# Zeroed rows from 112 partitions, single-batch scatters, and late weights loaded in portions, in a two-layer Flamingo block with two expert stages

## What is computed

```
x = x + tanh(g_xattn[0]) * masked_cross_attention(layernorm(x), ctx)     # 16 heads of 16
x = x + tanh(g_ffn[0])   * moe(layernorm(x))      # shared MLP + top 2 of 8 experts, F = 192
x = x + tanh(g_xattn[1]) * cross_attention(layernorm(x), ctx)
x = x + tanh(g_ffn[1])   * lora_ffn(layernorm(x)) # F = 1024, the top 1 of 8 low-rank corrections
```

## Time and profile before

| | |
|---|---|
| median of 3 runs | 944.09 us (935.59 to 944.37) |
| the profiled execution's own time | 942.44 us |
| its span | 940.4 us |
| PE busy | 789.5 us, 84% |
| DVE busy | 584.5 us, 62% |
| ACT busy | 469.9 us, 50% |
| POOL busy | 223.2 us, 24% |
| mean granted TensorE clock | 0.923 of full speed |
| moved by DMA | 118.91 MB, 126 GB/s over the span |

### The profile page before, as it was taken

The page is one execution under the profiler, slowest core; times in us unless marked ns, Lnnn a source line. Parts: engine busy times, 40 slices in busy tenths (PEclk is TensorE's granted clock), DMA queues, the critical chain, the costliest instruction groups (busy, mean ns, idle before and its releaser), DMA issues.

```text
span 940.4 us, 22247 instructions
## 1 busy us (share of the span) xinstructions
PE 789.5 (84%) x7992; PEld 612.4 (65%) x7992; DVE 584.5 (62%) x1773; ACT 469.9 (50%) x1004; POOL 223.2 (24%) x213
## 2 busy tenths in 40 slices
PE   5479999999989878604999858999999999878996
PEld 3247777776767655403899526767777777547996
DVE  4867777777767556501544547877888877663332
ACT  3336565564545346201566225655666665634543
POOL 2535222343233126001000535423231212000000
PEclk9789999999989789856999978999999999989998
DMA  7966788787767622112332696888879887000001
GB/s 198 227 167 137 159 173 163 150 176 172 136 135 158 158 66 81 49 48 61 98 123 92 186 189 137 171 179 167 193 152 181 167 178 146 10 2 1 18 18 35
DMA packets 152137, 118.91 MB, mean 126 GB/s; under 512 B 80844, under 2 KB 143608, under 8 KB 152024
## 3 DMA queue, kind: packets, MB, share of 16 engines
q1 hardware_dynamic: 144960, 107.35, 51.7%
q0 software_dynamic: 4096, 6.57, 2.6%
q10 hardware_dynamic: 2976, 3.61, 1.3%
HBM read 77.84 MB, written 39.40 MB: 125 GB/s over the span
## 4 chain that ended last, share of the span: by engine, by line
PE 62%; DMA 10%; DVE 9%; SPq 7%; issue 5%; ACT 4%; POOL 1%; another core or an unknown queue 0%; DVEq 0%; ACTq 0%; POOLq 0%
PE ps L1885 18%; PE ps L1998 8%; PE ps L2024 8%; PE ps L2047 6%; PE ps L2057 6%; SPq L610 4%; PE ps L2043 3%; DMA cT<-in_ctxT 3%; PE ps L2081 3%; DVE mx L1513 2%; DMA scr_x<-yt 2%; DMA QS<-scr_q 2%; DMA QS<-mp 1%; ACT prob L950 1%; PE ps L2067 1%
## 5 line engine op out<-in xcount | busy, mean ns | idle before, releaser
L950 ACT ACTIVATE prob<-ps 128x400 f32<-128x400 f32 (+1 forms) x384 | 183.0, 500 | 109.3 <-PE ps L2047 94.5
L2024 PE MATMUL ps<-KS,QS 96*100 96x361 bf16 x512 | 168.0, 343 | 24.3 <-DVE mx L1509 10.5
L1509 DVE CUSTOM_DVE_ANT_0 ps<-ps,biasq 100x361 f32<-100x361 f32 x256 | 135.9, 543 | 68.8 <-PE ps L2024 59.2
L1513 DVE TENSOR_REDUCE mx<-ps 100x1 f32<-100x361 f32 x256 | 127.0, 527 | 49.5 <-PE ps L2024 44.2
L2047 PEld LDWEIGHTS ps<-QS,KS 98*128 98x128 bf16 x1536 | 110.6, 101 | 51.7 <-issue 11.9
L2047 PE MATMUL ps<-QS,KS 98*128 98x100 bf16 x1536 | 135.1, 212 | 6.6 <-ACT prob L950 4.6
L1998 PE MATMUL ps<-cT,wk 128*128 128x361 f32 x256 | 102.5, 512 | 19.5 <-DMA ident<-in_ident 9.7
L2024 PEld LDWEIGHTS ps<-KS,QS 96*100 96x100 bf16 x512 | 65.1, 128 | 61.1 <-DVE mx L1509 17.7
L2057 PE MATMUL ps<-prob,V 128*17 128x100 f32 (+1 forms) x3072 | 82.6, 257 | 1.8 <-ACT xT L860 0.9
L689 POOL TENSOR_TENSOR kp<-kr,kp 128x722 bf16<-128x722 f32 x32 | 48.4, 1514 | 150.1 <-ACT kp L921 150.1
L2057 PEld LDWEIGHTS ps<-prob,V 128*17 128x17 f32 (+1 forms) x3072 | 67.0, 100 | 15.9 <-issue 10.8
(11 more groups left out here) (226 smaller groups left out, 1630.8 us busy)
## 6 DMA issues: line engine op xcount, KB each, us to landing
scr_k<-kp SPq DMA_DIRECT2D x96, 180.5 KB
KS<-scr_k SPq DMA_DIRECT2D x64, 270.8 KB, 3.6
cT<-in_ctxT SPq DMA_DIRECT2D x32, 361.0 KB
KS<-scr_k SPq DMA_DIRECT2D x64, 180.5 KB, 4.0
QS<-scr_q SPq DMA_DIRECT2D x64, 150.0 KB, 4.4
KS<-scr_k SPq DMA_DIRECT2D x64, 90.2 KB, 4.1
scr_q<-qp SPq DMA_DIRECT2D x24, 200.0 KB, 3.6
scr_q<-qp SPq DMA_DIRECT2D x48, 100.0 KB, 5.0
```

Of the source, the lines that this page charges most:

```text
L950: nc.scalar.activation(prob[0:KROWS[t], t, hg, :], ps[0:KROWS[t], c % 2, 0:HQ * S], ACT.Exp).then_inc(a["exp"], 1)
L1509: nc.vector.tensor_tensor_reduce(ps[0:S, banks[h % len(banks)], 0:S2], ps[0:S, banks[h % len(banks)], 0:S2], biasq[p][:, :], 1.0, -3.0e38, ...
L1513: nc.vector.reduce_max(mx[:, h:h + 1], ps[0:S, banks[h % len(banks)], 0:S2], axis=AX.X).then_inc(a["max"], 1)
L2024: mm(ps[0:S, banks[h % len(banks)], 0:S2], QS[p][0:SROWS, h, :], KS[p][0:SROWS, h * S2:(h + 1) * S2], start=True, stop=True).then_inc(a["s ...
```

## The change

The zeroed rows are written from 112 partitions with 3 rows each (336 rows) in place of 82 with 4 (328), and regions are 16 rows longer. `later_weights` moves behind `zero_fill` on SP. `scatter` takes one batch (two transfers). Batches 0 to 7 go out in POOL's loop for n = 8 to 15, each behind a wait for the end of step n-2, and `k3(n+1)` moves ahead of `biasT_(n)` in every round of the loop. The loads of `wiT`, `woT` and `BT` leave ACT; SP issues them in portions in steps 2 to 8 of attention 1 (two of 512 KB, four of 256 KB, then three of 128 KB), between the first half of the query load and `max_load`. `combine(1)` moves behind the last item. The counts that wait for the last weights follow (`NWF1`).

```diff
-REGION = B * S + TM
+REGION = B * S + TM + 16
...
-        ZROWS = 2 * S + TM
-        ZPART = 82
+        ZPART = 16 * 7
+        ZROWS = 3 * ZPART
+        NWF1 = 3 + KT + NFT1 // 2 + LPROD
...
+            def last_weights(b):
+
+                if b < KT:
+                    sp.dma_start(wiT[:, b, :], io["wiT"][b * P:(b + 1) * P]).then_inc(s_wf[1], 16)
+                elif b < KT + NFT1 // 2:
+                    t = 2 * (b - KT)
+                    sp.dma_start(woT[:, t:t + 2, :], io["woT"].rearrange("(t p) n -> p t n", p=P)[:, t:t + 2, :]).then_inc(s_wf[1], 16)
+                elif b == KT + NFT1 // 2:
+                    for r in range(LPROD):
+                        sp.dma_start(BT[r * LR:(r + 1) * LR, :], io["loraBT"]).then_inc(s_wf[1], 16)
+
...
                         expert_down(weights, u)
+                    if l == 1 and b >= 2:
+                        last_weights(b - 2)
                     max_load(l, b + 1, 1 - u)
...
                 max_load(l, B - 1, 1)
-                if l == 0:
-                    later_weights()
...
             zero_fill()
+            later_weights()
             sp.wait_ge(s0["tab"], START + NTAB)
...
                     for n in range(2, B):
-                        if n % 2 == 1 and n >= 9:
-                            scatter((n - 9) // 2)
                         bias(n, n % 2, n // 2, False)
-                        biasT_(n, n % 2, False)
+                        if n >= 8:
+                            pool.wait_ge(sa[0]["sT"], START + 3 * NHG * (n - 1))
+                            scatter(n - 8)
                         if n + 1 < B:
                             k3(l, n + 1)
+                        biasT_(n, n % 2, False)
                         if n % 2 == 0 and n >= 4:
                             norm_pair(F0, n // 2 - 2)
                     norm_pair(F0, NPAIR - 2)
-                    for j in range(NPAIR - 4, NPAIR - 1):
-                        scatter(j)
+                    for b in range(B - 8, B - 2):
+                        scatter(b)
...
-            scatter(NPAIR - 1)
+            for b in range(B - 2, B):
+                scatter(b)
...
-            act.wait_ge(s0["y"], START + NI)
-            act.dma_start(wiT[:, :, :], io["wiT"].rearrange("(k p) n -> p k n", p=P)).then_inc(s_wf[1], 16)
-            act.dma_start(woT[:, :, :], io["woT"].rearrange("(t p) n -> p t n", p=P)).then_inc(s_wf[1], 16)
-            for r in range(LPROD):
-                act.dma_start(BT[r * LR:(r + 1) * LR, :], io["loraBT"]).then_inc(s_wf[1], 16)
             attn(1)
...
                         combine(0)
-                        combine(1)
                 if b == NI:
+                    combine(1)
                     pair_stats(0)
```

More of the change, by code:

```diff
@@ L805, in low_piece, with scatter @@
                 nc.gpsimd.tensor_tensor(lo, raw, hi.bitcast(F32), ALU.subtract).then_inc(s0["plo"], 1)
-            def scatter(j):
+            def scatter(b):
+                j = b // 2
                 pool.wait_ge(s0["rt"], START + routed(j + 1))
@@ L811, in scatter @@
                     pool.wait_ge(s_zero, 16 * (1 + E))
-                for b in (2 * j, 2 * j + 1):
-                    for c in range(2):
-                        nc.gpsimd.indirect_dma_start(scr_x, bass.IndirectOffsetOnAxis(posi[:, c, b:b + 1], 0),
-                                                     normalized(b), None).then_inc(s_scat, 16)
+                for c in range(2):
+                    nc.gpsimd.indirect_dma_start(scr_x, bass.IndirectOffsetOnAxis(posi[:, c, b:b + 1], 0),
+                                                 normalized(b), None).then_inc(s_scat, 16)
             attn(0)
@@ L1079, in attn @@
                         else:
-                            act.wait_ge(s_wf[1], 16 * (5 + LPROD))
+                            act.wait_ge(s_wf[1], 16 * NWF1)
                             high(s1, *EARLY[0][:2])
@@ L1962, in logits @@
                 if g == 0:
-                    pe.wait_ge(s_wf[1], 16 * (5 + LPROD))
+                    pe.wait_ge(s_wf[1], 16 * NWF1)
                 pe.wait_ge(sn["xT"], START + NORMS[2 * l + 1] + g + 1)
```

## The result

The changed kernel takes **900.64 us** (median of 4 runs, 894.97 to 903.28) against 942.97 for the kernel before beside it: a ratio of 0.9561, with a 95% interval of 0.9501 to 0.9621. The profiled execution took 903.28 us (span 901.4, mean granted clock 0.951), 39.2 less than that of before. The forecast was 886, range 873 to 904. Faster is right, and the time lies inside the range, but 15 us of the forecast 57 are missing.

The account below looks back on a forecast made before the run. One transfer shape on about two DMA engines bounds the stretch near 400 us, PE and its ring of waits the rest. Terms -43.6 - 12 - 1.5 - 2 - 1 + 3 = -57.1 from 942.4 give 885.3, stated as 886 us, range 873 to 904.

Parts of the forecast that it names:

- The zero fill: Before the first tile: zeroed rows land sooner, PE's 44.58 us gap shrinks to 1.0 us; -43.6 us.
- issue-bound: SP's queue: with 112 partitions on all engines, eight fills cost only issue and register reads, 13.8 us.
- The scatters: Attention 0, steps 7 to 14: two scatters as a step opens instead of four in mid-step; -12 us.
- the burst's excess: Attention 0, steps 7 to 13: 17.8 us over quiet steps, between all and none recoverable, two thirds taken.
- paid by count: Rival: every POOL transfer delays its neighbours equally wherever it stands, so the 12 us stay; 898 us, chance 0.13.
- The row taken as nearest: Attention 1: POOL issues gather pairs at the same place with no "remote" waits; basis for taking two thirds.
- The stall as step 15 opens: End of attention 0: PE's 4.52 us standstill shrinks as `later_weights` leaves that spot; -1.5 us, between 0 and -4.5.
- The start of attention 1: Moving `combine(1)` lets PE start earlier, -2 us; final weights leaving that stretch, -1 us.
- The portions: Attention 1, seven steps: 2.4 MB of final weights may delay `max_load`; +3 us, between 0 and +12.6.
- weights gone: Start of attention 1: 2.4 MB of final weights leave a stretch with DMA engines 1.00 busy; -1 us (0 to -5).
- `later_weights` behind the fill: SP's queue before the first tile: its loads land while POOL scatters; 0, at worst tiles 4.7 us later.
- what would show it: The prediction's list of signs in fills, first-tile gap, clock, attention steps and waits that would show it right or wrong.

Follow-up runs that it names:

- e1_fill: Kernel before with only the new zero fill (112 partitions, regions 16 rows longer): 875.04 us against 920.31 for the kernel before, ratio 0.9522.
- e6_84: Kernel before with its zero fill cut as 84 partitions of 4 rows instead of 82: 902.07 us against 939.00 (one run).
- e8_fill_late: Kernel before with the new fill, and the final weights in portions at the end of a step's loads: 897.71 us against 939.00, ratio 0.9560.
- e4_act: Changed kernel with the final weights loaded whole by ACT as attention 1 begins: 875.63 us against 920.31 for the kernel before, ratio 0.9536.
- e3_out: Changed kernel with all scatters moved behind the loop of steps of attention 0: 896.21 us against 920.31 for the kernel before (one run).
- e10: Changed kernel with k3 first, scatters after the last weighting, and final weights loaded whole by ACT: 876.25 us against 920.69, ratio 0.9511.
- e2_pv: Changed kernel with a step's two scatters waiting for the ended batch's last weighting, not its last transposed score: 884.96 us against 920.31, ratio 0.9630.
- e9: Changed kernel with k3 first on POOL, then the scatters after the ended batch's last weighting: 879.55 us against 920.69, ratio 0.9571.
- e5_again: Changed kernel run once more, unedited, in another set: 897.06 us against 939.00 for the kernel before, ratio 0.9559.
- e7_late: Changed kernel with the portions of the final weights asked for at the end of a step's loads: 901.84 us against 939.00, ratio 0.9592.
- e11_again: Changed kernel run a third time, unedited: 880.87 us against 918.68 for the kernel before, ratio 0.9500.

## Why the prediction was right, and where it was not

**The zero fill (-43.6 forecast): right.** Alone it is worth 45.3 us by the medians (e1_fill), and the stretch to the first tile is 47.2 shorter in the two traces. The step that carries it, that 112 partitions make the fill issue-bound, holds: eight fills took 9.95 us and not 13.8, since an issue is 0.58 and not 0.88 us and the rest of a fill 0.76 and not 0.85. The steps behind it fit by luck. The forecast had the landing release POOL at 382.6 and a gap of 1.0 us left on PE. In fact POOL started at 382.65 for its places, which were ready 1.2 us later than before, and no gap was left, since PE came free 1.0 us later too. Most of the other 2.6 us of the 47.2 is the clock, which the prediction left unpriced at up to 2: from the first tile to its down projection (9.2 us before, 6.8 now) it was 0.71 and is 1.00.

**The scatters (-12 forecast): wrong, +1.1 measured.** The step that failed is "the burst's excess": 17.8 us over quiet steps were read as a clash of four scatters in mid-step with the normalising instruction, of which two thirds would go. The place of the excess was read rightly: it lies in the steps with scatters, and DVE's and ACT's "remote" waits are part of it. What failed is that a change of order would take it away. The same instructions of before cost 136.4, 134.6 or 128.6 us in the costly sets and 121.3 in another, the changed ones 138.0 and 136.1 or 122.8. The kernel before and the changed kernel were both in the costly condition when they were compared, so the 15 us were there to see and were not gained. In the costly sets a scatter costs whichever order it stands in; the new order only moves the standstill from DVE, ACT and PE in mid-step to PE at the weighting. Within one set the old order is never the slower one: 136.4 against 138.0, 134.6 and 128.6 (e6_84, e8_fill_late) against 136.1 and 136.5, and 121.3 against 123.3 for e4_act's. The rival "paid by count" fits the first pair of traces, with (136.4 - 121.3) / 16 = 0.9 us a scatter in the old order and (138.0 - 122.8) / 14 = 1.1 in the new, and its 898 us are nearer to the 900.64 than the forecast. But e8_fill_late paid half of that in a costly set, and in the other sets the count costs next to nothing, at most 0.15 us a scatter (e4_act against e3_out). The row taken as nearest, the gathers of attention 1, said rightly that such a pair can be free, but nothing in one trace tells that its stalls are not the kernel's own.

**The stall as step 15 opens (-1.5): right in size, not in its reason.** It shrank by 0.8 in the row and by 1.0 in the stretch. But the move of `later_weights` isn't shown to have done it: in the costly sets the stall is 3.0 to 4.5 us with the loads there (before, e6_84, e8_fill_late) and 3.0 to 4.4 without them, and in the other sets it is 0.6 us in every kernel, e1_fill among them, which still has them there.

**The start of attention 1 (-3 for `combine(1)` and the weights): right in the row, not in the time.** PE's first projection came 0.51 us after its last item, 2.6 us better. But the normalised queries came later by 1.4 us (they waited for `xn`), and the stretch to the first transpose shrank by 0.4. Over the kernels, this stretch and attention 1 together take 280.1 to 282.6 us with `combine(1)` in its old place and weights whole (before, e1_fill, e6_84), and 281.4 and 282.3 with it moved (e4_act, e10): 0 us for the move. The first stretch alone is some 3 us shorter with it (37.8 and 38.0 against 40.7 to 41.5), as forecast, and attention 1 some 3 us longer (243.7 and 244.3 against 238.6 to 241.6). The prediction's own caution, that the gathered rows set the first queries, was priced at half a microsecond and took 1.4; why the rest comes back in attention 1 is open.

**The portions (+3): right in kind, low.** Kernels with whole weights take 280.1 to 282.6 us for the two stretches, five of them, mean 281.7; kernels with portions ahead of `max_load` take 282.9 to 289.7, seven of them, mean 286.4. That is +4.7, within the bounds of 0 and 12.6, and net of what the "weights gone" from the start bought (-1 forecast). It is a mean over sets: within one set the difference was 4.2 us (e2_pv and e3_out against e1_fill and e4_act), 3.2 (e9 against e10) and 0.3 (e5_again against e6_84), and the changed kernel by itself gave 288.5, 282.9 and 288.1 in its three traces. The mechanism named, the landing of the maxima behind the portion, shows at 3.69 and 3.35 us in the place of 1.93, but it is one of several: in e7_late the wait for the context grows instead.

**`later_weights` behind the fill (0): right**; e1_fill and e11_again both take 27.8 us to the first tile.

**Together:** -45 to -47 for the fill, +4.7 for the portions, +1 for the scatters, -1 for the stretch with the stall, 0 for the rest, some -41 against the -42.3 measured. The tail's +2.5 in the balance is no part of it: the kernels' tails lie between 131.3 and 135.4 us without order.

**The signs.** Of "what would show it", three held (fills under 15 us, a gap under 5 us with the clock at 1.00 from 400 to 425 us, the first projection within 1 us). Steps 7 to 13 at 119 to 128 us did not hold in the first trace, and did in e11_again. The steps of attention 1 grew by more than 1 us in two cases, and the wait for the maxima's load came as the sign of the portions' cost. Of "remote" waits at openings there were none; the stall named "issue" stood there instead.

## What to carry to other kernels

Where a transfer repeats one shape while all else waits, look at its partition count, and at the share of the DMA engines that it keeps busy, before its bytes. Moving bytes out of a quiet stretch into a ring of small dependent loads cost time in both places of the ring's queue that were tried. And before a stall is written down as the work of the order of instructions, have the same kernel traced in another set: here 15 us of stalls came and went with no edit. Times of two kernels from different sets can't be compared either, unless both have the kernel before beside them.

## What the hardware showed that was not expected

- While POOL issues scatters, other engines can stand nearly still. On PE 51 of 72 short multiplications go through at 24 ns each, then two or three in 0.7 us until the second scatter ends. With the scatters in mid-step DVE and ACT stop as well (5.7 and 5.5 us in steps 7 to 13 of the kernel before). It happened in two of five sets and there in each of the six traces, on one chip in one set and not in the other. In the two costly sets the kernel before took 943 and 939 us, in the others 918.7 to 920.7. Steps 7 to 13 (136.4 against 121.3) and the stretch from the last transpose to the first down projection (32.9 against 25.7) hold 22.3 us of that difference, with e1_fill's trace in place of the kernel before's. What about a set makes it so is not known. That PE ran out of instructions (e2_pv's theory A) is not shown: it was argued from the place where the standstill bites, and no instruction packet was under way there.
- A two-input operation on POOL (128x722, 1.47 us) holds a DVE instruction (a factor on 100x16) of 0.17 us until it is over and a little longer: 0.43 to 0.59 us where they overlapped in e11_again, up to 2.24 where it followed upon a scatter. The same instruction within a scatter took 0.17.
- From 82 to 84 partitions the eight fills go from 46.62 to 17.06 us of SP's queue, and to 9.95 with 112.
